# Summed transposes of two relu tiles: fp32 matmuls against an identity become TensorE's transpose mode, in a fused state-space and expert layer

## What is computed

```python
# state-space block, on layernorm(x)
u_inner = u @ W_in.T + b_in                  # 256 -> 2 * 512
x, z = jnp.split(u_inner, 2, axis=-1)
dbc = x @ W_x.T + b_x                        # delta (16), B (16), C (16)
delta = softplus(dbc[..., :16] @ W_dt.T + b_dt)
h = h * exp(delta * A) + x * (delta * B)     # over time, 512 x 16 states
y = (sum_n h * C + x * D) * silu(z)
x1 = x0 + y @ W_out.T + b_out
# expert block, on layernorm(x1)
scores = softmax(x1n @ Wg.T + bg); top 2 of 4 give w
base = x1n @ Wi.T                            # 256 -> 1024
hidden = relu(base + lora_e)                 # per expert e
out = x1 + sum_e w_e * (hidden_e @ Wo.T)     # 1024 -> 256
```

## Time and profile before

| what | value |
|---|---|
| runs | 1985.83, 1981.93, 1984.35 us; median 1984.35 |
| profiled execution | 1996.33 us, span 1994.5 us |
| mean granted TensorE clock | 0.936 of full speed |
| busy: VectorE, GpSimd | 91%, 90% |
| busy: TensorE, ScalarE | 86%, 71% |
| 12 bodies in the steady part, 343.39 to 1734.93 us | 1391.54 us, 116.0 us each |

### The profile page before, as it was taken

The page is one execution under the profiler, slowest core; times in us unless marked ns, Lnnn a source line. Parts: engine busy times, 40 slices in busy tenths (PEclk is TensorE's granted clock), DMA queues, the critical chain, the costliest instruction groups (busy, mean ns, idle before and its releaser), DMA issues.

```text
span 1994.5 us, 27643 instructions
## 1 busy us (share of the span) xinstructions
PE 1719.9 (86%) x7776; PEld 934.9 (47%) x7776; DVE 1823.7 (91%) x2246; ACT 1422.9 (71%) x2755; POOL 1793.7 (90%) x780
## 2 busy tenths in 40 slices
PE   3365769898998989899898989989898998988999
PEld 1112225555544545454454555445455544545565
DVE  2799999999999999999999999999999999999941
ACT  3566767778687777868777787877778787776633
POOL 1999999999999999999999999999999999999800
PEclk8676779999999999999999999999999999999999
DMA  5546462653546365454636545463654546365100
GB/s 178 137 103 150 117 148 77 154 132 97 128 110 164 80 158 126 101 126 110 164 81 160 124 102 122 110 164 88 156 121 111 117 106 164 82 153 121 37 19 14
DMA packets 146769, 235.05 MB, mean 118 GB/s; under 512 B 22064, under 2 KB 46896, under 8 KB 146096
## 3 DMA queue, kind: packets, MB, share of 16 engines
q1 hardware_dynamic: 146608, 233.18, 48.5%
HBM read 190.11 MB, written 42.99 MB: 117 GB/s over the span
## 4 chain that ended last, share of the span: by engine, by line
DVE 26%; POOL 24%; issue 21%; PE 20%; ACT 5%; DMA 1%; SPq 0%; DVEq 0%; POOLq 0%; ACTq 0%
POOL hs L1344 12%; DVE decay L1286 11%; POOL hs L1356 7%; DVE hs L1276 6%; DVE hs L1286 4%; PE bank L932 4%; PE bank L868 3%; PE y_ps L946 3%; PE bank L910 2%; POOL e_dt L1334 2%; PE bank L884 2%; PE bank L927 2%; POOL z_dt L1323 1%; ACT decay L1089 1%; ACT xin L1047 1%
## 5 line engine op out<-in xcount | busy, mean ns | idle before, releaser
L1344 POOL TENSOR_TENSOR hs<-dx_rep,b_rep 128x2048 f32<-128x2048 f32 x256 | 1161.0, 4538 | 31.4 <-PE y_ps L946 19.2
L1286 DVE TENSOR_TENSOR_SCAN decay<-decay,state,hs 128x512 f32<-128x512 f32 x640 | 797.2, 1274 | 37.8 <-ACT decay L1089 33.9
L1089 ACT ACTIVATE decay<-dt_rep,a_sb 128x512 f32<-128x512 f32 x1024 | 694.3, 686 | 29.0 <-DMA dt_rep<-rep_scratch 10.6
L1286 DVE TENSOR_TENSOR_SCAN hs<-decay,state,hs 128x512 f32<-128x512 f32 x384 | 487.6, 1270 | 4.6 <-ACT decay L1089 3.0
L1356 POOL TENSOR_TENSOR hs<-hs,c_rep 128x1024 f32<-128x1024 f32 x192 | 454.7, 2368 | 4.1 <-ACT state L1103 4.1
L1276 DVE TENSOR_TENSOR hs<-decay,c_rep 128x1024 f32<-128x1024 f32 x320 | 384.7, 1202 | 0.0
L946 PE MATMUL y_ps<-hs,nsum 128*32 128x512 f32 x2048 | 299.6, 660 | 56.7 <-DVE gated L1179 27.7
L868 PE MATMUL bank<-xn_t,w_in_sb 128*128 128x512 f32 x512 | 254.4, 627 | 12.0 <-DVE silu L1174 7.4
L910 PE MATMUL bank<-w_i_sb,x_t 128*128 128x512 f32 x492 | 247.9, 627 | 13.8 <-DVE x L1190 9.2
L1103 ACT COPY state<-decay 128x2 f32<-128x2 f32 x320 | 51.0, 159 | 287.1 <-DVE hs L1276 287.0
L927 PE MATMUL bank<-ident,r 128*128 128x128 f32 x1840 | 230.8, 279 | 21.6 <-DVE x L1190 20.4
(11 more groups left out here) (149 smaller groups left out, 1750.6 us busy)
## 6 DMA issues: line engine op xcount, KB each, us to landing
dx_rep<-rep_scratch SPq DMA_DIRECT2D x256, 256.0 KB, 4.7
dt_rep<-rep_scratch SPq DMA_DIRECT2D x256, 256.0 KB, 7.6
b_rep<-bc_scratch SPq DMA_DIRECT2D x256, 64.0 KB, 3.3
rep_scratch<-z_dt SPq DMA_DIRECT2D x64, 256.0 KB, 2.5
rep_scratch<-e_dt SPq DMA_DIRECT2D x64, 256.0 KB, 2.7
c_rep<-bc_scratch SPq DMA_DIRECT2D x256, 64.0 KB, 2.2
xin<-in_u SPq DMA_DIRECT2D x16, 512.0 KB, 4.0
xr<-in_u SPq DMA_DIRECT2D x16, 512.0 KB, 4.3
```

The lines of the kernel that those rows point to most:

```text
L1089: nc.scalar.activation(decay[:, j, :], dt_rep[m % 2][:, j, :], ACT.Exp, scale=a_sb[:, J * s + j:J * s + j + 1]).then_inc(decay_ready, 1)
L1286: v.tensor_tensor_scan(hs[s % 4][:, j, :] if kept else decay[:, j, :], decay[:, j, :], hs[s % 4][:, j, :], state[:, b, n:n + 1], ALU.mult, ...
L1344: nc.gpsimd.tensor_tensor(hs[s % 4][:], dx_rep[m % 2][:], b_rep[:, k, :].unsqueeze(1).to_broadcast([P, J, T]), ALU.mult).then_inc(input_re ...
```

## The change

The L927 matmuls get `is_transpose=True`: the eight calls of a T job stay the same, with `r1`'s block first and `r2`'s added to it in the bank. The tables of all five engines are written anew for steady bodies, last body and end. No job is added or dropped; T0 of a chunk moves from step 15 of its "post" body to step 0 of its "late" body. The diff, cut to the rows that matter here:

```diff
@@ -49,61 +49,61 @@
 PE_SIDE = [
-    "S1 late, J2 late | S2 late",
-    " | J3 late, T1 late",
-    "S3 late, A0 pre | K0 late",
-    "F0 post, T2 late | A1 pre, F1 post, F2 post, E0 main, F3 post",
-    " | B0 pre, T3 late, B1 pre",
-    "J4 late | B2 pre",
+    "T0 late, S1 late, J2 late | J3 late, T1 late",
+    "S2 late | ",
+    "S3 late, K0 late, A0 pre | F0 post, T2 late",
+    "A1 pre, F1 post | F2 post, E0 main",
+    "F3 post | B0 pre, T3 late, J4 late, B1 pre",
+    " | B2 pre",
     "B3 pre, S4 late, E1 main | ",
...
 ACT_SIDE = [
...
-    "J4 late |  | B2 pre, B3 pre | S4 late, E1 main",
-    " |  | R2 post, V1 main | W1 main, Z1 main",
...
+    " |  | B2 pre, B3 pre | S4 late",
+    " | E1 main | V1 main | R2 post, W1 main, Z1 main",
...
 DVE_SIDE = [
...
     "K0 late, F0 post |  |  | ",
-    " | F1 post | F2 post | F3 post",
-    "S0 main | P0 post |  | ",
-    "Y0 main |  |  | P1 post",
-    " |  |  | S1 main",
+    " | F1 post | F2 post | S0 main",
+    "F3 post | P0 post |  | Y0 main",
+    " |  | P1 post | ",
+    " |  | S1 main | ",
...
 PE_END = [
...
-    " | J6 post, T5 post, J7 post, S6 post",
-    " | K2 post, S7 post, T6 post",
-    " | T7 post, K3 post",
...
+    "S6 post, S7 post, K2 post | T6 post",
+    "T7 post, K3 post | ",
 ]
...
@@ -925,7 +925,7 @@
                         for f in range(4):
                             for r in (r1, r2):
                                 mm = pe.matmul(ps[:, f * P:(f + 1) * P], r[i % 2][:, f * P:(f + 1) * P], ident[:],
-                                               start=r is r1, stop=r is r2)
+                                               start=r is r1, stop=r is r2, is_transpose=True)
```

More of the change, by code:

```diff
@@ L51 @@
 PE_SIDE = [
-    "S1 late, J2 late | S2 late",
-    " | J3 late, T1 late",
-    "S3 late, A0 pre | K0 late",
-    "F0 post, T2 late | A1 pre, F1 post, F2 post, E0 main, F3 post",
-    " | B0 pre, T3 late, B1 pre",
-    "J4 late | B2 pre",
[6 rows of a table added]
     "B3 pre, S4 late, E1 main | ",
-    "J5 late, C0 pre | ",
-    "S5 late | D0 pre, K1 late",
[2 rows of a table added]
     "T4 late, E2 main, D1 pre | T5 late",
     "G0 post, G1 post | H0 post",
[L63 to L67, removed]
[5 rows of a table added]
 ]
@@ L122 @@
     "",
-    "",
-    "V0 pre, U0 pre",
+    "V0 pre",
+    "U0 pre",
     "W0 post",
@@ L133 @@
     "",
+    "",
     "K0 late",
-    "",
     "",
@@ L151 @@
 PE_LAST = [
-    " | S1 late",
-    "J2 late | S2 late, T1 late",
-    "F0 post, J3 late | S3 late, E0 main",
-    "K0 late | T2 late, F1 post, F2 post",
-    " | F3 post",
-    "J4 late, T3 late | S4 late, E1 main",
-    "K1 late, T4 late | J5 late",
-    " | S5 late",
-    "E2 main, T5 late | ",
-    "G0 post | G1 post",
-    "J6 late, H0 post, S6 late | K2 late",
-    "J7 late | S7 late, T6 late",
-    "T7 late | K3 late, I0 post",
+    "T0 late, S1 late | J2 late",
+    " | T1 late, E0 main",
+    "S2 late, F0 post, J3 late | K0 late",
+    "S3 late | T2 late, F1 post",
+    "F2 post | ",
+    "F3 post, T3 late, E1 main, J4 late | S4 late",
+    "K1 late, T4 late | ",
+    "J5 late | S5 late, T5 late",
+    "E2 main | ",
+    "G0 post | ",
+    "G1 post, J6 late, H0 post, S6 late, K2 late | ",
+    "J7 late | S7 late, T6 late, T7 late",
+    "K3 late | I0 post",
     "E3 main, J0 post | S0 post, J1 post, T0 post",
-    "S1 post | T1 post, J2 post",
-    "K0 post | S2 post",
+    "S1 post | T1 post, J2 post, K0 post",
+    " | S2 post",
 ]
 ACT_LAST = [
[16 rows of a table removed]
[16 rows of a table added]
 ]
@@ L194 @@
     "F0 post |  |  | ",
[3 rows of a table removed]
[3 rows of a table added]
     " |  | Y0 main | ",
[6 rows of a table removed]
[6 rows of a table added]
     " |  |  | ",
     " |  |  | ",
[1 row of a table removed]
[1 row of a table added]
 ]
 POOL_LAST = [
-    "V1 main",
     "",
     "",
+    "V1 main",
     "",
@@ L238 @@
     "",
-    "",
-    "",
-    "K2 late, K3 late",
-    "",
-    "K0 post",
+    "K2 late",
+    "K3 late, K0 post",
+    "",
     "",
@@ L338 @@
     "",
-    "K2 late",
-    "",
-    "K3 late",
-    "",
-    "K0 post",
-    "K1 post, K2 post, K3 post",
     "",
@@ L347 @@
     "",
+    "K3 late, K0 post",
+    "",
+    "K1 post",
+    "",
+    "",
+    "",
+    "K2 post, K3 post",
 ]
```

## The result

The change runs in 1965.3 us (median of 4 runs, 1962.75 to 1968.13); the kernel before, run beside it on the same chip, in 1985.09 us (median of 4, 1981.93 to 1997.83). The ratio is 0.9889 [0.9843, 0.9934]: 19.8 us less. The forecast was 1956 us, a gain of 28 us on the median, so it was 9 us too low, inside its range. The profiled executions differ by more than the medians: 1996.33 against 1968.13 us, spans 1994.5 against 1966.3 us. That is 28.2 us, and the sum of the prediction, which was made against that execution, said 28.8 (29 before rounding to the median).

What follows compares the result with a forecast made beforehand. VectorE and GpSimd were taken to bound the steady bodies, TensorE the end. Gains of 19.5 (steady), 2 (last body) and 7.3 us (end) sum to 29, giving a median of 1956 us, 8-in-10 range 1936 to 1973.

Steps and rivals of the forecast that it cites:

- The T job: TensorE's transposes: transpose mode takes a job from 2.0 to 1.0 us, or leaves 2.0 at the other end.
- Rival 4: Transpose mode is no faster when adding into a bank, jobs stay 2.0 us: 1973 us; chance 0.05.
- K0 and F0: Steady body: K0 issued ahead of A0 and the sum removes VectorE's 0.33 us wait and 1.2 of 1.52.
- The decay of step 7: Steady body: E1 now behind two decays on ScalarE, so VectorE's whole 0.69 us wait goes.
- GpSimd: Steady body: its 1.71 us wait for a state sum goes; its 1.29 us for the layer norm's root stays.
- The 1.5 us a body: Steady bodies: net gain after small new waits, bounds 0 and 2.5 us; 13 bodies give 19.5 us.
- rival 1: Steady bodies: nearly all waits go, 2.5 to 3 us a body: 1937 us; chance 0.12.
- rival 3: TensorE's added idle time makes its clock fall further; slower, 2000 us; chance 0.07.
- Rival 3's point of decision: Steady bodies: the clock decides from about 2.2 us of new waits a body on.
- The last body: Up to 1908 us: with 8 us less on TensorE some VectorE waits go, 2 us, bounds 0 and 4.
- the end: After the last body, TensorE's: six shorter transpose jobs and waits gone give 7.3 us, bounds 3 and 9.
- the 12 us: Offset of the runs shown below the profiled execution, 12.0 us, used to carry 1967.5 to a median of 1955.5.

Runs made afterwards that it cites:

- e10: The kernel before with K0 issued ahead of A0 and the sum, F0 behind the sum, plain matmuls, other orders old; 2023.75 us, ratio 1.0179.
- e7: The change with K0 and F0 issued where they were, K0 behind A0 and the sum; 1990.49 us, ratio 0.9999.
- e8: The change with the gate's E1 on ScalarE put back ahead of step 7's first two decays; 1968.1 us, ratio 0.9899.
- e4: The change with zero-weight 512-column matmuls added ahead of D2, J1 and H0, where TensorE waits; 1957.46 us, ratio 0.9839.
- e0: The kernel before, unchanged, run for a second trace and more times; 1991.67 us, ratio 1.0009.
- e2: The change's new tables with plain fp32 matmuls for the T jobs, without the transpose flag; 1978.18 us, ratio 0.9939.
- e3: The change with the old tables of the last body and the end, T0 put at their head; 1970.57 us, ratio 0.9905.
- e1: The kernel before with the transpose flag alone, old tables kept; 1993.92 us, ratio 1.0028.
- e9: The kernel before with the transpose flag and the new tables of the last body and the end, old steady tables; 1993.04 us, ratio 1.0028.

## Why the prediction was right or wrong

**The T job** (1.0 us taken, 2.0 as the other end) is right: 1.07 us, and adding into a bank costs nothing. Rival 4 is out. TensorE's busy time fell by 91 us where "about 110 us or more" stood. The saving of 0.93 us a job makes 112 for the 120 jobs; part of the difference came back as pieces at low clock (L910 at 3.78 us), the rest was not traced.

**K0 and F0** (0.33 and 1.2 to 1.52 us) are right in what goes and incomplete in what it rests on. Both waits went entirely. The move was argued on TensorE alone; e10 shows that without the rest of the tables it costs 36 us, and e7 that without the move these tables give nothing in the steady bodies. Its worth in the finished order, 1.7 us a body, is more than the whole 1.5 that was taken for a body.

**The decay of step 7** (0.69 us) was mis-sized: 0.2 to 0.35 us by e8. The prediction let the wait of before stand for what E1's old place would cost in the new order. There VectorE comes to that decay 0.5 us later, so most of the wait goes with or without the move.

**GpSimd**: the 1.71 us went, as argued. "The 1.29 us for the root stay" did not hold, and it matters that they vary: 0.7 to 1.0 us in a short body and 2.2 to 2.5 in a long one, and 0.25 to 1.7 in e4's (3.2 once). So the root's wait is no fixed cost of GpSimd. That it takes up what VectorE and ScalarE are late by is a reading; no run shows it.

**What eats some of it.** The 1.5 us a body came out as 1.6, by two things that cancel: a short body of the change is 113.4, 2.5 us less than before (rival 1's figure), and the long ones, with more time at the lower clock, give back 0.9 us on the mean. The prediction held these apart as rivals with 0.12 and 0.07; they happened together, and that 1.6 lies next to 1.5 is luck. One ground given for rival 3 was read too narrowly: ahead of the fall at 1860 us stood not only eight transposes and the router's products but between them a product of 512 columns (L910, 1.88 us at 1856.09). Rival 3's point of decision, 2.2 us of new waits, was not reached: VectorE's new waits in a long body are 0.30 + 0.66 + 0.18 us.

**The last body** (2 us) and **the end** (7.3 us) gained 8.2 together, 1.1 less than the sum. How they share it depends on the cut: by the windows above 2.0 and 6.2, by the end of VectorE's last product (1907.47 before, 1886.34 in the change) 1.1 and 7.1. T7's and K2's waits went as said; against it stand K3's wait, 0.3 us longer, S7's new 0.47, which the prediction didn't have, and 0.93 instead of 1.0 a job. The end's length, "about 79", is 80.3.

**From the trace to the median**: this step failed, and it is nearly the whole miss. The prediction took the 12 us by which the runs shown lay below the profiled execution as an offset that would stay. It does not: the change's profiled execution lies 2.8 us above its median, and e0's, e2's and e3's lie 3.2, 2.8 and 0.5 above theirs. The kernel before itself runs from 1978 to 1998 us, and 1996.33, at a clock of 0.936, was near the top of that. Against the medians of before in the three groups (1985 to 1990 us) the change gains 20 to 25 us. e0 gives a reason for such a spread, a body of 113.9 where the clock holds and 116.0 where it falls, and the mean clocks of the 68 timed runs bear it out; no profile of a fast execution confirms it.

**What the mean body hides.** Three kinds of kernel with different waits (before, e1 and e9, e7) all have bodies of 116.0 to 116.1 us. Their traces show that this is hardly chance: the falls of the clock come back 116.05 us apart (in e1 in every body, at 496.70, 612.75, 728.80, 844.86, 960.91 and so on), also where one body is longer (116.55) and the next shorter (115.76). In the change they come back every 228.69 us, over one long and one short body (931.12, 1159.81, 1388.51, 1617.20), and so in e8 and in most bodies of e3. So bodies and falls keep step, and the steady gain is a change from one step to another. Which of the two leads, no run shows. It means that a mean body is a poor price for a single wait: e8 and the change have the same step, e7 and the kernel before too. Why the clock fell at 1860 us in the kernel before stays open.

## What to carry to other kernels

Time taken off an engine that is not the bound turns into idle time, and on TensorE idle time can cost the clock: the faster instruction alone gained nothing here, the new orders alone 0.6%, both 1.1%, and a few zero-weight products put exactly where TensorE waits anyway some 0.4% more. A job's place has to be priced on every engine that waits for what is pushed back behind it, not only on its own, and with the buffers that a new order hands out. And a sum made against one profiled execution should be carried to a median only after a second profile of the same kernel has shown where the first lies in the spread.
